# A graph-convolution kernel on one core: first chunk in one transfer, chunk 2 turned by halves, one row sum on VectorE, and two products of x moved among the first slots

## What is computed

```
h = jnp.maximum(_layernorm(x, axis=-1), 0.0)
rowsum = adj.sum(axis=1)
d_inv_sqrt = jnp.where(rowsum > 0, rowsum ** (-0.5), 0.0)
normalized_adj = d_inv_sqrt[:, None] * adj * d_inv_sqrt[None, :]
support = normalized_adj @ h
out = jnp.maximum(support @ W + b, 0)
return x + out
```

## Time and profile before

| | |
|---|---|
| runs before | 393.49, 393.66, 393.80 us |
| median | 393.66 us |
| the profiled execution | 393.01 us |
| its span | 391.2 us |
| TensorE busy | 383.5 us |
| VectorE busy | 317.9 us |
| ScalarE busy | 288.7 us |
| moved by DMA | 151.86 MB |

### The profile page before, as it was taken

The page is one execution under the profiler, slowest core; times in us unless marked ns, Lnnn a source line. Parts: engine busy times, 40 slices in busy tenths (PEclk is TensorE's granted clock), DMA queues, the critical chain, the costliest instruction groups (busy, mean ns, idle before and its releaser), DMA issues. The chain is left out here.

```text
span 391.2 us, 5139 instructions
## 1 busy us (share of the span) xinstructions
PE 383.5 (98%) x1754; PEld 319.9 (82%) x1754; DVE 317.9 (81%) x312; ACT 288.7 (74%) x286; POOL 115.0 (29%) x253
## 2 busy tenths in 40 slices
PE   8998999999999999999999999999999999999995
PEld 8886888888888888888888888888888888888884
DVE  6839966899686899958689995868899497889996
ACT  2889898788787878679878867978886793346533
POOL 2470335653121226114235811422520144000000
PEclk9999999999999999999999999999999999999999
DMA  7999999999999999999999999999999965997665
GB/s 296 427 421 426 426 424 427 425 429 428 422 423 424 427 427 429 420 426 424 424 428 426 428 419 428 425 425 427 428 426 429 404 229 220 394 372 255 214 169 207
DMA packets 24216, 151.86 MB, mean 388 GB/s; under 512 B 3328, under 2 KB 3328, under 8 KB 7552
## 3 DMA queue, kind: packets, MB, share of 16 engines
q1 hardware_dynamic: 24192, 151.55, 94.5%
HBM read 147.33 MB, written 4.22 MB: 387 GB/s over the span
## 5 line engine op out<-in xcount | busy, mean ns | idle before, releaser
L441 ACT ACTIVATE hi<-at,s 128x1024 fp32r<-128x1024 f32 x112 | 122.9, 1144 | 44.5 <-issue 32.5
L928 PE MATMUL moved<-hi,G 128*128 128x512 f32 x384 | 149.6, 390 | 1.5 <-DVE acc L729 1.5
L930 PE MATMUL moved<-hi,G 128*128 128x512 f32 x384 | 149.4, 389 | 0.0
L929 PE MATMUL moved<-lo,G 128*128 128x512 f32 x384 | 149.4, 389 | 0.0
L713 DVE SCALAR_TENSOR_TENSOR lo<-at,s,hi 128x1024 fp32r<-128x1024 f32 x112 | 140.8, 1278 | 9.1 <-ACT hi L441 9.1
L732 DVE TENSOR_TENSOR acc<-moved,acc 128x1024 f32<-128x1024 f32 x84 | 102.7, 1223 | 50.5 <-PE moved L930 50.5
L431 ACT ACTIVATE nat<-nat 128x2048 f32<-128x2048 f32 x64 | 122.1, 1908 | 7.8 <-DMA nat<-in_adj 7.8
L928 PEld LDWEIGHTS moved<-hi,G 128*128 128x128 f32 x384 | 72.1, 188 | 17.0 <-DVE acc L729 1.9
L930 PEld LDWEIGHTS moved<-hi,G 128*128 128x128 f32 x384 | 72.1, 188 | 15.0
L929 PEld LDWEIGHTS moved<-lo,G 128*128 128x128 f32 x384 | 72.1, 188 | 14.9
L601 POOL TENSOR_TENSOR row_sum<-part 128x1 f32<-128x1 f32 x32 | 17.9, 561 | 183.2 <-ACT nat L431 183.0
(11 more groups left out here) (75 smaller groups left out, 253.3 us busy)
## 6 DMA issues: line engine op xcount, KB each, us to landing
nat<-in_adj SPq DMA_DIRECT2D x64, 1024.0 KB, 13.8
at<-in_adj_t SPq DMA_DIRECT2D x64, 1024.0 KB, 12.4
acc<-in_x SPq DMA_DIRECT2D x4, 512.0 KB, 7.1
nat<-d_dram SPq DMA_DIRECT2D x2, 1024.0 KB, 5.8
nat<-in_x_t SPq DMA_DIRECT2D x4, 512.0 KB, 6.0
turned<-in_x_t SPq DMA_DIRECT2D x4, 512.0 KB, 6.9
out<-nat SPq DMA_DIRECT2D x4, 512.0 KB, 5.1
turned<-in_x SPq DMA_DIRECT2D x3, 512.0 KB, 14.7
```

Source lines behind the costliest of these rows:

```text
L441: nc.scalar.activation(hi[g % RING][:, 2 * c:2 * c + 2, :], at[g % LA][:, 2 * c:2 * c + 2, :], ACT.Copy, scale=s[:, j:j + 1]).then_inc(hi_ ...
L928: nc.tensor.matmul(into[:, f, :], big, hi[g % RING][:, t, :], start=begins, stop=False)
L929: nc.tensor.matmul(into[:, f, :], big, lo[g % RING][:, t, :], start=False, stop=False)
L930: mm = nc.tensor.matmul(into[:, f, :], small, hi[g % RING][:, t, :], start=False, stop=ends)
```

## The change

- The first chunk of x comes in one transfer of 512 KB on one semaphore instead of two of 256 KB. VectorE waits for all of it. SP issues W second.
- TensorE multiplies nine times by zeros at the start instead of eight.
- Chunk 2 is turned and copied by halves, between the projections of chunk 1, and W is rounded between the two copies.
- Block 3 of adj is summed by VectorE (`sum_early`) instead of ScalarE. Whoever waits for sums now waits for two counters.
- ScalarE's order: the sums of blocks 0, 1 and 2 stand one work step later than before, block 3's is gone, and chunk 3's high part of G is made between the two tiles of slot 0.
- GpSimd makes the second scale before the rstd of chunks 1 to 4.
- VectorE makes chunk 3's low part of G after the first low tile, takes the first panel after three low tiles instead of four, and makes chunk 4's low part of G one place later.

```diff
-WARM = 8
+WARM = 9
-AT_ONCE = {0: 1, 1: 2}
+AT_ONCE = {0: 1, 1: 2, 2: 2}
+BY_VECTOR = (3,)
...
-            eng.wait_ge(nat_summed, m + 1)
+            dve_part = len([e for e in BY_VECTOR if e <= m])
+            at_least(eng, nat_summed, m + 1 - dve_part)
+            at_least(eng, dve_summed, dve_part)
...
-            half = BW // 2
-            sp.dma_start(h(0)[:, 0:half, :], x[0][:, 0:half, :]).then_inc(x_first, DMA)
-            sp.dma_start(h(0)[:, half:BW, :], x[0][:, half:BW, :]).then_inc(x_landed[0], DMA)
+            load_x(0)
             sp.dma_start(w_sb[:, :, :], w).then_inc(w_landed, DMA)
...
             scale_of(0)
-            rstd_of(1)
-            rstd_of(2)
             scale_of(1)
+
+            for c in range(1, AHEAD):
+                rstd_of(c)
...
+            def sum_early(m):
+                dve.wait_ge(nat_landed[m % LN], DMA * (m // LN + 1))
+                nc.vector.reduce_sum(part[:, m // 2, m % 2:m % 2 + 1], nat[m % LN][:, :],
+                                     axis=mybir.AxisListType.X).then_inc(dve_summed, 1)
...
+            take_stats(3)
+            rest_of_raw(0)
+            take_stats(4)
+            rest_of_w()
+            rest_of_raw(1)
+            sum_early(3)
+            rest_of_raw(2)
             rest_of_turned(AHEAD - 1)
-            for n in range(4):
-                subtract(n // 2, n % 2)
+            subtract(0, 0)
             rest_of_raw(AHEAD - 2)
-            piece = 4
+            subtract(0, 1)
+            subtract(1, 0)
+            piece = 3
             for g, (k, q, panels) in enumerate(SLOTS):
                 if NARROW[k] and NARROW[SLOTS[g + 2][0]]:
                     for p in range(2):
                         gather(k, 2 * q + p)
-                        if (g, p) == (2, 0):
+                        if (g, p) == (2, 1):
                             rest_of_raw(AHEAD - 1)
-                            continue
-                        for n in range(piece, 2 * g + p + 5):
+                        upto = 2 * g + p + (4 if g < 3 else 5)
+                        for n in range(piece, upto):
                             subtract(n // 2, n % 2)
-                        piece = 2 * g + p + 5
+                        piece = upto
...
-            for c, n in ((1, 3), (2, 2), (3, 1)):
-                if n:
-                    project(c, range(n))
+            project(1, range(2))
+            turn_part(2, 0)
+            project(1, range(2, 3))
+            turn_part(2, 2)
+            project(1, range(3, 4))
+
+            for c, n in ((2, 2), (3, 1)):
+                project(c, range(n))
                 turn(c + 1)
                 project(c, range(n, BW))
```

More of the change, by code:

```diff
@@ L266, in build @@
         nat_summed = sem("nat_summed")
+        dve_summed = sem("dve_summed")
         s_ready = sem("s_ready")
@@ L507, in add_b @@
                                          bias=b_sb[:, f:f + 1]).then_inc(b_added, 1)
[L509 to L514, removed]
-                if c == 2:
[L517 to L528, removed]
+            for c in range(OWN):
+                if c == 2:
+                    round_raw(0)
+                for t in range(0, BW, AT_ONCE[c]):
+                    take_part(c, t)
+                    if (c, t) == (2, 0):
+                        round_w()
+            sum_nat(0)
+            round_raw(1)
+            take_turned(3)
+            sum_nat(1)
+            round_raw(2)
+            take_high(4)
+            sum_nat(2)
+            round_tile(0, 0)
+            round_raw(AHEAD - 2)
+            round_tile(0, 1)
             round_slot(1)
-            round_raw(AHEAD - 2)
             round_raw(AHEAD - 1)
@@ L641, in take_stats @@
                 for t in tiles:
-                    if c == 0 and t == 0:
-                        dve.wait_ge(x_first, DMA)
-                    if t == (BW // 2 if c == 0 else 0):
+                    if t == 0:
                         dve.wait_ge(x_landed[c], DMA)
@@ L779, in _ @@
                 measure_and_centre(c, second)
-            for c in range(OWN, AHEAD):
-                take_stats(c)
-                if c == AHEAD - 1:
-                    rest_of_w()
-                rest_of_raw(c - 3)
-            rest_of_raw(AHEAD - 3)
+            take_stats(3)
[5 more added lines that the diff above has]
+            rest_of_raw(2)
             rest_of_turned(AHEAD - 1)
-            for n in range(4):
-                subtract(n // 2, n % 2)
+            subtract(0, 0)
             rest_of_raw(AHEAD - 2)
-            piece = 4
+            subtract(0, 1)
+            subtract(1, 0)
+            piece = 3
             for g, (k, q, panels) in enumerate(SLOTS):
@@ L851, in turn_part @@
             def turn_part(c, t):
-                if c == 1 and t > 0:
-                    pe.wait_ge(hT_ready, 1)
+                if c == 0:
+                    at_least(pe, part_hT_ready, part_before(c, t) - 2)
+                elif t == 0:
+                    pe.wait_ge(part_hT_ready, part_before(c, t) - 1)
                 else:
-                    at_least(pe, part_hT_ready, part_before(c, t) - (2 if c == 0 else 1))
+                    pe.wait_ge(hT_ready, c)
                 for tile in range(t, t + AT_ONCE[c]):
```

4 lines of the change are left out of this document (1 added, 3 removed).

## The result

| | before | after |
|---|---|---|
| runs beside each other | 15 | 15 |
| median | 393.63 us | 396.25 us |
| lowest, highest | 393.35, 394.85 us | 394.67, 399.39 us |
| granted clock of TensorE, mean over a run | 0.997 to 1.000 (the 23 runs beside e1) | 0.989 to 0.999 |
| profiled execution, its span | 393.01, 391.2 us | 395.02, 393.2 us |

One run before took 652.58 us and is not counted as its highest. The ratio is 1.0076 (95% interval 1.0056 to 1.0097): slower, by 2.6 us, where 1.05 were forecast. The runs after fall into three groups by clock. Four at 0.998 or more took 394.67 to 395.79; eight at 0.993 to 0.995 took 395.95 to 397.69; three at 0.989 or 0.990 took 398.58 to 399.39. The profiled execution is of the first group.

The account below looks back on a forecast made before the run. TensorE's start was taken as the bound, followed at slot 3: 28.2 + 5.71 + 11.02 + 2.7 = 47.65 against 46.60, +1.05. That put the profiled execution at 394.05 and, with 0.65 added, the median at 394.7 us (393.9 to 395.5).

Parts of the forecast that it names:

- Part 4: Chunk 4's low part of G behind position 5's copy: TensorE waits for it at slot 3, loss 2.7 us.
- Part 1: First chunk in one transfer, nine zero products: adj's fourth block lands 0.25 us earlier, at 20.55.
- Part 2: Chunk 2 by halves, one block's sum on VectorE: slot 0 begins at 28.2 us instead of 28.30.
- Part 3: Chunk 3's G amid slot 0: slot 1 begins 5.71 us after slot 0 instead of 7.28, gain 1.57.
- the time is set by when TensorE gets going: Whole kernel: whatever moves the start of slot 3 (46.60 us) moves the end by as much.
- nothing that lies behind slot 3: Behind slot 3: nothing there can give back a shift of its start; no TensorE wait after 46.60 could grow.
- Rival A: At slot 3, no new wait for chunk 4's G: slot 3 at 44.93 us, -1.67, time 392.0; chance 0.10.
- The sum: Start of slot 3: 28.2 + 5.71 + 11.02 + 2.7 = 47.65 us against 46.60, +1.05.
- the 0.65 between the profiled execution and the median of before: Whole time: median 393.66 is 0.65 us above the profiled execution's 393.01, added to the forecast 394.05.

Follow-up runs that it names:

- e1: The changed kernel again, unaltered, for its spread and a second trace: 396.4 us, ratio 1.0077.
- e2: The changed kernel with chunk 4's low part of G back between the copies of positions 4 and 5: 394.33 us, ratio 1.0016.
- e8: The changed kernel with chunk 4's G back between those copies, the first chunk in two transfers and eight zero products: 393.72 us, ratio 0.9996.
- e6: The changed kernel with ten products of zeros in TensorE's wait at slot 3: 394.84 us, ratio 1.0031.
- e12: The changed kernel with ten zero products in the wait at slot 3 and five more ahead of chunk 4's product: 394.68 us.
- e16: The changed kernel with one more low tile on VectorE ahead of chunk 4's G, lengthening the wait at slot 3: 398.3 us.
- e7: The kernel before with only chunk 3's G amid slot 0, chunk 4's in its old place: 393.92 us, ratio 1.0004.
- e3: The kernel before with only chunk 4's low part of G moved behind the copy of position 5: 397.19 us, ratio 1.009.
- e5: The kernel before with chunk 4's G behind the copy of position 5 and ten zero products in the wait at slot 3: 395.82 us, ratio 1.005.
- e14: The kernel before with only the twelfth block of adj loaded and summed one slot later: 393.52 us, ratio 0.9992.
- e18: The kernel before with only every block of adj from the twelfth on one slot later, up to slot 20: 393.56 us, ratio 1.0.

## Why the prediction was right in its direction and wrong in its size

394.7 was forecast, 396.25 measured, above the range of 393.9 to 395.5.

The step that failed is the price of Part 4, "2.65, and 0.1 for the slow first matmul": it puts the matmuls behind the new wait at full speed. The runs showed that TensorE's clock falls to 1.2 GHz after most of these waits, which costs 1.6 us more. The landing of the fourth block in Part 1 failed too, and is smaller in the result. Part by part:

- **Part 1** failed in its step "The fourth block then lands at 20.55 (19.7 to 20.8)". The reduction began at 21.60, 21.14 and 22.21 (after, e1, e2), and at 21.59 with two transfers (e8), each time right after a wait for that block. I had taken one duration to landing, of one execution, as if it were a property of the block. Over the twenty profiles it lands between 20.6 and 22.2, and the 20.8 of the earlier trace rows is among the earliest. The mean is 21.2 with two transfers and 21.3 with one: neither the gain of the single transfer nor a loss by it shows in the landing.
- **Part 2** followed from it: slot 0 at 29.20 and 28.74 in the profiles of the changed kernel (after, e1), not 28.2. In the other profiles with the same start it begins at 29.71 (e2), 28.85 (e6), 28.87 (e12) and 28.19 (e16); in e16 the block landed early, the reduction began at 20.69, and the forecast's 28.2 came out. The reduction itself took 2.29, where I took 2.28; from its start to chunk 4's product there are 4.70 us, as the step has it (25.3 - 20.55 = 4.75). ScalarE's high part began at 22.81 in the profile after, not 22.1, so that with an early block slot 0 would not have come as early as 27.6.
- **Part 3**: 5.61 instead of 7.28, a gain of 1.67 where 1.57 was forecast. But "the time is set by when TensorE gets going" was an overstatement that this change's own new wait hid: without that wait the gain is lost in slot 6, to a wait that "nothing that lies behind slot 3" had ruled out (e7, e8). Rival A, 392.0 if the wait at slot 3 weren't there, was wrong in the same way: e2, which is that case, took 394.33, with slot 3 only 0.27 earlier than before, since slot 0 began at 29.71, and a new wait of 0.9 behind it; in e8 slot 3 is 0.87 earlier and slot 7 0.92 later.
- **Part 4**: a wait of 2.45 and a slow first matmul. Slot 3 comes 8.05 after slot 2 instead of 5.45, +2.6, and slot 4 another 0.13 late: 2.7, as forecast. What the term lacked is the price behind the wait: "2.65, and 0.1 for the slow first matmul" leaves out that TensorE's clock falls after most such waits. That is 1.6 us of the result (396.4 - 394.84, e1 and e6; 1.4 by e3 and e5); without it the changed kernel takes 394.84, inside the range.
- **The sum.** The runs without a fall, 394.67 to 395.79, and e12's 394.68 lie where 394.7 was put. That is partly luck: slot 0 was 0.5 to 1.0 later than forecast, and against that the 0.65 between the profiled execution and the median of before should not all have been added. In the profiles of e14 and e18, which share before's order up to slot 3, slot 0 is at 28.84 and 28.69 and slot 3 comes 5.92 and 5.79 after slot 2, with a wait of 0.3 and 0.2 for the same G. In the late order that wait is part of the long one and doesn't come on top. This account of the 0.65 is argued from the profiles; no run tests it. (Two slips change nothing: the terms of the sum add up to 47.63, not 47.65, and five matmuls, not six, follow the one at 32.54.)

## What to carry to other kernels

Price a new wait of the matmul engine twice: its length, and the stretch at 1.2 GHz that may follow it; runs that differ by more than before, with different mean clocks, are its sign. When a start is made earlier, look for the resource that is next, and look for it in the windows: where the DMA share is 1.00 through the whole stretch, as here, suspect that a landing depends on the bytes ahead of it in the queue, and test it by moving a load. Where an edit that should pay does not, put the load of the next bound later instead of taking the edit back; the two may be worth nothing apart and all of it together. And take the time of a landing from several profiles: here it moved by 1.5 us between executions whose starts are the same program (20.7 to 22.2).

## What I had not expected of the hardware

- In e1 and e3 the clock fell after a standstill of 2.45 us, and only after work had gone on again; it stayed at 1.2 GHz for about eight matmuls back to back. In e16, with a standstill of 4.53 us, it fell before the work went on. Eleven of 15 runs of the changed kernel have the mean clock of such a fall. The 1.52 us wait of the kernel before left it at 0.997 or more in every run. But three of e7's twelve runs, with a wait of 1.86 and none longer, are at 0.993 to 0.996. In the profiles with a mean of 0.997 or more the clock is below full nowhere between 24 and 384 us; what they lack lies at the very end.
- Zeros are enough to keep it: twenty passes of 128 columns in e5.
- The DMA queue is full at 421 to 431 GB/s in every 4 us window from 48 to 68 us of e7. 1 MB is 2.46 us of that; two blocks of adj and one slot's block together 7.4, against TensorE's 5.44 a slot, and this is what slots 1 and 4 ask for (slot 0 asks for one slot's block more). One and one are 4.9, so that the backlog melts by only 0.5 a slot:

```profile
60.00:64.00 4.00, 4.00 (x19) 3.32 (x18) 1.42 (x2) 3.35 (x5) 1.08 (x5) 1.00 1.01 426
64.00:68.00 4.00, 2.14 (x10) 1.47 (x9) 3.45 (x3) 3.56 (x4) 3.52 (x8) 1.00 1.01 428
```

  The Trainium skill (DMA: Bandwidth & Descriptors, Where 436 GB/s comes from) puts the ceiling on the side of SBUF at 435 GB/s and says that for loads from HBM a limit of about 358 GB/s for a core binds. The trace agrees with the first figure and exceeds the second (426 and 428 GB/s in the two rows, all from one core).
